# Grouped-query scores of a fusion model: four row groups of TensorE instead of block-diagonal keys

## The chip, the cores and the metric

The kernel runs on one core of one Trainium2 chip. The metric is the device time of one launch in microseconds; where several executions are given it is their median. Beside it stands one execution taken with the profiler.

## What is computed

A model of four layers over 32 sequences of 68 tokens (36 image patches and 32 text tokens), 256 wide, all in float32. Each layer has a mixing block and a feed-forward block, each behind a layer norm and with a residual sum. The change touches the mixing block of the last layer, grouped-query attention with 16 query heads and 4 key and value heads of 16 dimensions. Its core in the reference:

```python
Q = (x @ Wq.T).reshape(B, S, HKV, G, HEAD_DIM)
K = (x @ Wk.T).reshape(B, S, HKV, HEAD_DIM)
V = (x @ Wv.T).reshape(B, S, HKV, HEAD_DIM)
...
scores = jnp.einsum('bskgd,bswkd->bskgw', Q, K_win) * scale
...
attn = jax.nn.softmax(scores, axis=-1)
out = jnp.einsum('bskgw,bswkd->bskgd', attn, V_win)
return out.reshape(B, S, HQ * HEAD_DIM) @ Wo.T
```

The window reaches 128 tokens to both sides, more than the 68 there are, so each token sees all of its sequence and nothing is masked.

After it come the router and the dense expert block of the last layer.

## The kernel before, in words

There are five engine programs that meet only at semaphores. TensorE's order of steps is written out by a planner: `step(...)` puts a step into `pe_order`, and `Banks.plan` gives each result one of the eight PSUM banks in turn and notes which semaphore count frees that bank; `wait_free` waits for it. The ring `A` has banks 0 to 5, `B` 6 and 7, `W8` all eight.

Sequences ("batches") are grouped in five chunks of 7, 7, 6, 6 and 6. For each chunk `kv3` (L1043) and `q3_` (L1058) form keys, values and queries for all its batches; ScalarE copies them out of PSUM (`keep_kv3`, `keep_q3`, L1342 and L1360). Heads are padded from 16 to 32 rows, so that the four key heads fill 128 partitions, and the four queries of each key head stand side by side: 4 x 68 = 272 queries for each key head. Keys go into `kblk`, a block-diagonal tile: for each batch 4 x 68 columns of which head g fills only rows 32g to 32g+31, and the rest is zero, set once by GpSimd.

For each batch b:

1. `s3` (L1064, matmul at L1070): the 272 queries are cut into three pieces of 91 (from 0, 91 and 181, so the last two overlap by one). One matmul for each piece, 91 x 272, contracts over all 128 rows, for all four heads at once, because of the zeros in `kblk`. Each has a bank of ring `A`.
2. `shift3` on VectorE (L1862 to L1870): for each piece the maximum over the 68 keys (L1867), and the subtraction (L1868) into `p3`.
3. `exp3` on ScalarE (L1371), `sum3` on VectorE (sum L1876, reciprocal L1877), and GpSimd multiplies by the reciprocal (L2007).
4. `pT3_` (L1074, transposes at L1079): twelve transposes on TensorE; ScalarE copies each piece into `pT3` (a helper at L1130).
5. `pv3` (L1083, matmul at L1089): four matmuls, one for each key head, on column groups of the array (`tile_position=(0, g * HPAD)`); ScalarE copies the result (`keep_o3`).
6. `out3` at a chunk's end (helper at L759) multiplies by the output weights; VectorE adds to `h` and starts the layer norm.

`AHEAD` is 3, and `p3` has four slots. The orders of the turn b: TensorE does pT3(b), s3(b+3), pv3(b), with the projections of the next chunk or `out3` between at some turns. ScalarE does keep_o3(b-1), the three copies of pT3(b), exp3(b+3). VectorE does shift3(b+3), sum3(b+2). GpSimd works in order of b. Each float32 matmul is two passes in the trace, a transpose is one.

Of the kernel before, what the change touches and what calls it, by code (L numbers as in the profile page):

```python
# [13 lines left out]
P = 128  # L14
D = 256
HALVES = D // P
BATCH = 32
# [44 lines left out]
PROWS = 91  # L62
PIECE0 = [0, 91, 181]
AHEAD = 3

# [33 lines left out]
def build(nc, t, out):  # L99
# [3 lines left out]
    with ExitStack() as ctx:  # L103
# [197 lines left out]
        kblk = carve(KR * KV_HEADS * SEQ).rearrange("p (b g s) -> p b g s", g=KV_HEADS, s=SEQ)  # L301
# [42 lines left out]
        AB = Banks(psum, [0, 1], tenants)  # L344
        Q = Banks(psum, [0, 1, 2, 3], tenants)
# [7 lines left out]
        ln_ring = {L0A: F, L0F: Q, L1A: Q, L3A: W8}  # L353
# [183 lines left out]
        def plan_qkv3(c):  # L537
            A.plan(("k3", c), (sem("k3_kept"), c + 1))
            for j in range(V3[c]):
                A.plan(("v3", c, j), (sem("v3_kept"), V30[c] + j + 1))  # L540
            step("kv3", c)
            for j in range(GROUP):
                A.plan(("q3", c, j), (sem("q3_kept"), GROUP * c + j + 1))
# [13 lines left out]
        for b in range(BATCH + 1):  # L557
            if b in FEED3:
                plan_qkv3(FEED3[b])
            if b < BATCH:  # L560
                for i in range(PIECES):
                    A.plan(("pT3", b, i), (sem("pT3_kept"), PIECES * b + i + 1))
                step("pT3", b)
            if b + AHEAD < BATCH:
                plan_s3(b + AHEAD)
            if b and (b == BATCH or b in CHUNK_B0):
                c = CHUNKS - 1 if b == BATCH else CHUNK_B0.index(b) - 1
                plan_h("out3", L3A, c)
                plan_ln_after(L3F, c, 2)
            if b < BATCH:  # L570
                B.plan(("o3", b), (sem("o3_kept"), b + 1))
                step("pv3", b)
# [150 lines left out]
        def _(pe):  # L723
# [319 lines left out]
            def kv3(c):  # L1043
# [3 lines left out]
                dst = A.wait_free(pe, ("k3", c))  # L1047
                product(dst[:, 0:ntok(c)], lambda k: wk3[:, k, :], lambda k: xn[:, k, chunk(c)],
                        HALVES).then_inc(sem("k3_done"), 1)
                for j in range(V3[c]):  # L1050
                    dst = A.wait_free(pe, ("v3", c, j))
# [6 lines left out]
            def q3_(c):  # L1058
                for j in range(GROUP):
                    dst = A.wait_free(pe, ("q3", c, j))  # L1060
# [3 lines left out]
            def s3(b):  # L1064
                c = chunk_of[b]
                pe.wait_ge(sem("q3_kept"), GROUP * (c + 1))
                pe.wait_ge(sem("k3_kept"), c + 1)
                for i in range(PIECES):
                    dst = A.wait_free(pe, ("s3", b, i))
                    pe.matmul(dst[0:PROWS, 0:KV_HEADS * SEQ],  # L1070
                              q3[:, c % 2, b - CHUNK_B0[c], PIECE0[i]:PIECE0[i] + PROWS], kblk[:, at3(b)],
                              start=True, stop=True).then_inc(sem("s3_done"), 1)

            def pT3_(b):  # L1074
                pe.wait_ge(sem("p3_ready"), b + 1)
                for i in range(PIECES):
                    dst = A.wait_free(pe, ("pT3", b, i))
# [5 lines left out]
            def pv3(b):  # L1083
                c = chunk_of[b]
                pe.wait_ge(sem("v3_kept"), V30[c + 1])
                dst = B.wait_free(pe, ("o3", b))
# [6 lines left out]
            def out3(c):  # L1093
                pe.wait_ge(sem("o3_kept"), CHUNK_B0[c] + CHUNK_BATCHES[c])
                into_h("out3", wo3, lambda k, cols: oT3[:, k, cols], c, GROUP)
# [11 lines left out]
        def _(act):  # L1107
# [232 lines left out]
            act.wait_ge(sem("pool_setup"), 6)  # L1340

            def keep_kv3(c):  # L1342
                act.wait_ge(sem("k3_done"), c + 1)
                if c >= 2:
                    act.wait_ge(sem("s3_done"), PIECES * CHUNK_B0[c - 1])
                    act.wait_ge(sem("o3_done"), CHUNK_B0[c - 1])
                src = A.at(("k3", c))
                for g in range(KV_HEADS):
                    rows = slice(g * HPAD, (g + 1) * HPAD)
                    ins = act.activation(kblk[rows, at3(CHUNK_B0[c]):at3(CHUNK_B0[c]) + CHUNK_BATCHES[c], g, :],  # L1350
                                         seqs(src[rows, 0:ntok(c)]), ACT.Copy)
                ins.then_inc(sem("k3_kept"), 1)
                for j in range(V3[c]):
# [3 lines left out]
                    copy(vb3[0:SEQ, at3(b):at3(b) + n, :], A.at(("v3", c, j))[0:SEQ, 0:n * P].rearrange("p (b n) -> p b n", n=P),  # L1357
                         "v3_kept")

            def keep_q3(c):  # L1360
                for j in range(GROUP):
                    act.wait_ge(sem("q3_done"), GROUP * c + j + 1)
                    if c >= 2 and j == 0:
                        act.wait_ge(sem("s3_done"), PIECES * CHUNK_B0[c - 1])
                    copy(q3[:, c % 2, 0:CHUNK_BATCHES[c], j * SEQ:(j + 1) * SEQ], seqs(A.at(("q3", c, j))[:, 0:ntok(c)]),
                         "q3_kept")

            def exp3(b):
                act.wait_ge(sem("s3_shifted"), PIECES * (b + 1))
# [3 lines left out]
            def keep_o3(b):  # L1373
# [4 lines left out]
                     B.at(("o3", b))[:, 0:GROUP * SEQ].rearrange("p (j t) -> p j t", j=GROUP), "o3_kept")  # L1378

            keep_kv3(0)  # L1380
            keep_q3(0)
            for b in range(AHEAD):
                exp3(b)
            for b in range(BATCH + 1):
# [7 lines left out]
                for i in range(PIECES):  # L1392
# [3 lines left out]
                         A.at(("pT3", b, i))[0:SEQ, 0:KV_HEADS * PROWS].rearrange("p (g q) -> p g q",  # L1396
                                                                                 g=KV_HEADS)[:, :, -lap:PROWS],
# [10 lines left out]
        def _(dve):  # L1408
# [691 lines left out]
```

## Time and profile before

| | |
|---|---|
| median of 3 runs | 1849.72 us (1848.54 to 1851.34) |
| profiled execution | 1853.17 us |
| its span, first to last instruction | 1851.4 us |
| TensorE busy over the span | 1680.1 us, 91% |
| VectorE busy | 798.7 us, 43% |
| ScalarE busy | 498.6 us, 27% |
| GpSimd busy | 418.0 us, 23% |
| the last attention block | about 1494.8 to 1702.8 us of the span |

The shares are means over some twenty stages with different limits. The block of the change is about an eleventh of the span, so it has to be read by itself, from the timeline and the tables of stretches. PE is TensorE's matmuls, PEld its loads of weights, which run beside them. A matmul's own duration holds its latency; of matmuls in a row the distance between two starts is the price.

### The profile page before, as it was taken

The numbers are of one execution on the slowest core, as the hardware profiler recorded it, in microseconds if no ns is written. First come the engines' busy times: TensorE is split into PE (matmuls) and PEld (weight loads), VectorE is DVE, ScalarE is ACT, GpSimd is POOL, SyncE is SP. The second block draws the span as 40 slices with busy tenths as digits, with TensorE's granted clock in tenths as the row PEclk, the third lists the DMA queues.
The fourth block names the chain that finished last, engine by engine and source line by source line (L and its number), as shares of the span: only waits on it lengthen the run. The fifth ranks groups of instructions, "written<-read, shape, count | busy, mean of one in ns | idle before, by whom it ended". The sixth has DMA issues, their size and how long they took to land.

```text
span 1851.4 us, 22690 instructions
## 1 busy us (share of the span) xinstructions
PE 1680.1 (91%) x8028; PEld 1167.6 (63%) x8028; DVE 798.7 (43%) x1698; ACT 498.6 (27%) x962; POOL 418.0 (23%) x430
## 2 busy tenths in 40 slices
PE   5877499988999999999949999999899989998999
PEld 4532134437999999999935555776864456667444
DVE  3531499987111111111126760122456555675455
ACT  1234344541212221212116323123110035543000
POOL 0363577771111111211121000000100012232000
PEclk8989799997899999999989979999579999998999
DMA  5233434434344344404161000010000010000000
GB/s 168 66 94 95 110 106 96 101 71 150 146 160 175 150 160 159 162 28 160 33 182 39 1 1 28 1 46 1 1 1 0 1 46 1 1 1 1 12 17 20
DMA packets 59046, 129.17 MB, mean 70 GB/s; under 512 B 10563, under 2 KB 39268, under 8 KB 52388
## 3 DMA queue, kind: packets, MB, share of 16 engines
q1 hardware_dynamic: 54996, 116.96, 19.8%
q0 software_dynamic: 3936, 10.75, 1.7%
q8 instruction: 64, 1.05, 0.2%
q14 instruction: 50, 0.41, 0.1%
HBM read 196.35 MB, written 9.97 MB: 111 GB/s over the span
## 4 chain that ended last, share of the span: by engine, by line
PE 75%; DVE 10%; SPq 5%; issue 4%; POOL 3%; ACT 2%; DMA 1%; DVEq 0%; ACTq 0%; POOLq 0%
PE psum L727 39%; PE psum L1030 13%; PE psum L759 7%; PE psum L822 4%; SPq L627 3%; DVE work L1734 3%; PE psum L737 2%; PE psum L1009 2%; PE psum L938 2%; DVE work L1868 1%; SPq L624 1%; DVE work L1867 1%; POOL xn L1937 1%; ACT work L1130 1%; PE psum L1039 1%
## 5 line engine op out<-in xcount | busy, mean ns | idle before, releaser
L727 PE MATMUL psum<-work 128*128 128x128 f32 (+3 forms) x3400 | 470.4, 300 | 16.1 <-DMA work<-in_xp 15.9
L727 PEld LDWEIGHTS psum<-work 128*128 128x128 f32 x3400 | 440.0, 193 | 33.5 <-DMA work<-in_xp 15.9
L1030 PE MATMUL psum<-w_late,xn 128*128 128x512 f32 x544 | 242.0, 603 | 0.0
L1801 DVE TENSOR_TENSOR work<-sq,psum 128x512 f32<-128x512 f32 x82 | 56.3, 687 | 387.3 <-PE psum L727 387.3
L1030 PEld LDWEIGHTS psum<-w_late,xn 128*128 128x128 f32 x544 | 103.5, 193 | 128.6 <-issue 119.2
L822 PE MATMUL psum<-work,xn 128*128 128x408 f32 (+1 forms) x320 | 152.9, 591 | 31.9 <-POOL work L1959 31.4
L1734 DVE TENSOR_TENSOR_SCAN work<-psum,work 128x414 f32<-128x414 f32 (+1 forms) x160 | 158.8, 1058 | 43.2 <-POOL work L1959 38.9
L1959 POOL TENSOR_TENSOR work<-work 128x408 f32<-128x408 f32 (+1 forms) x160 | 160.9, 1039 | 58.0 <-PE psum L822 29.6
L1918 POOL TENSOR_TENSOR rs<-rs,power 128x4 f32<-128x4 f32 (+3 forms) x40 | 44.6, 1115 | 547.2 <-DVE rs L1428 540.9
L1618 DVE SCALAR_TENSOR_TENSOR h<-psum,gate,h 128x256 f32<-128x256 f32 x272 | 119.4, 480 | 106.8 <-PE psum L1030 104.1
L1130 ACT ACTIVATE work<-psum 68x364 f32<-68x364 f32 (+10 forms) x256 | 108.0, 463 | 139.5 <-PE psum L727 57.5
L822 PEld LDWEIGHTS psum<-work,xn 128*128 128x128 f32 x320 | 55.2, 200 | 125.3 <-POOL work L1959 81.1
L1225 ACT ACTIVATE psum<-work,a_neg 128x408 f32<-128x408 f32 (+1 forms) x160 | 100.3, 627 | 122.6 <-DVE work L1734 122.6
L1985 POOL DMA_INDIRECT y_rows<-sq,row_of x41 | 40.5, 987 | 367.0 <-ACT sq L1130 367.0
L1464 DVE TENSOR_TENSOR h<-h,psum 128x512 f32<-128x512 f32 (+1 forms) x45 | 29.4, 654 | 159.1 <-PE psum L759 122.8
L1126 ACT ACTIVATE xn<-psum 128x512 f32<-128x512 f32 (+1 forms) x63 | 34.4, 574 | 224.9 <-PE psum L737 224.7
L1267 ACT ACTIVATE sq<-psum 128x512 f32<-128x512 f32 x82 | 49.0, 597 | 161.1 <-PE psum L727 161.0
L938 PE MATMUL psum<-w_attn 128*128 128x512 f32 x128 | 62.4, 632 | 22.2 <-POOL w_attn L1928 22.2
L2007 POOL TENSOR_TENSOR work<-work 91x816 f32<-91x816 f32 x32 | 49.5, 1548 | 139.3 <-DVE work L1877 139.3
L727 PE MATMUL psum<-work,w_attn 128*128 128x408 f32 (+1 forms) x200 | 74.3, 531 | 2.5 <-ACT work L1123 2.5
L1130 ACT ACTIVATE sq<-psum 128x256 f32<-128x256 f32 x41 | 15.7, 383 | 185.8 <-PE psum L727 185.8
L737 PE MATMUL psum<-ident,sq 128*128 128x128 f32 x238 | 43.7, 332 | 24.3 <-DVE sq L1449 23.6
(266 smaller groups left out, 2052.9 us busy)
## 6 DMA issues: line engine op xcount, KB each, us to landing
work<-in_W SPq DMA_DIRECT2D x123, 1024.0 KB
work<-c_rows SPq DMA_DIRECT2D x48, 204.0 KB, 3.1
w_attn<-in_B SPq DMA_DIRECT2D x64, 128.0 KB, 2.4
work<-c_rows SPq DMA_DIRECT2D x32, 238.0 KB, 3.2
w_attn<-in_A SPq DMA_DIRECT2D x64, 64.0 KB, 2.2
w_attn<-in_A SPq DMA_DIRECT2D x32, 128.0 KB, 2.5
work<-in_A SPq DMA_DIRECT2D x32, 128.0 KB, 2.5
work<-y_rows SPq DMA_DIRECT2D x8, 512.0 KB, 7.8
```

The source lines that it names most:

```text
L727: mm = pe.matmul(dst, lhs(k), rhs(k), start=(k == 0), stop=(k == parts - 1))
L737: tr = pe.transpose(dst[:, at:at + P], src[:, k * P:(k + 1) * P], ident[:])
L759: mm = pe.matmul(cols, lhs(k, slice(i * P, (i + 1) * P)), w[:, k, :], start=(k == 0), stop=(k == parts - 1 and bias is None))
L822: pe.matmul(dst[:, 0:ntok(c)], diag[:, m, n, :], ym[:, g % RING, 0:ntok(c)], start=(n == 0), stop=(n == N_STATE - 1)).then_inc(sem("y_adde ...
L938: mm = pe.matmul(banks[m], unit_short(i)[:, m * P:(m + 1) * P], unit_long(i), start=first_mm, stop=last_mm)
L1030: mm = pe.matmul(dst.rearrange("p (e n) -> p e n", e=2), xn[:, k, i * P:(i + 1) * P], w_last[:, 2 * q:2 * q + 2, k, :], start=(k == 0), st ...
L1130: act.activation(dst, src, ACT.Copy).then_inc(sem(signal), 1)
L1225: act.activation(dst[:, :, 1:SEQ + 1], seqs(dtx[:, m, chunk(c)]), ACT.Exp, scale=a_neg[:, m, n:n + 1]).then_inc(sem("decay"), 1)
L1618: dve.scalar_tensor_tensor(h[:, i], W8.at(("dx", r, i, q))[:, e * D:(e + 1) * D], gate[:, 5, i, 2 * q + e:2 * q + e + 1], h[:, i], ALU.mul ...
L1734: dve.tensor_tensor_scan(f_buf[:, g % RING, 0:N], AB.at(("a", g))[:, 0:N], added, 0.0, ALU.mult, ALU.add).then_inc(sem("scanned"), 1)
L1801: dve.tensor_tensor(hm[:, j % 2, 4 * q:4 * q + 4, :].rearrange("p k n -> p (k n)"), sa[:, i % 2], A.at(("e3", j, q)), ALU.mult).then_inc(s ...
L1959: pool.tensor_tensor(seqs(ym[:, g % RING, 0:ntok(c)]), f[:, :, 1:SEQ + 1], seqs(cbr[:, k % CRING, 0:ntok(c)]), ALU.mult).then_inc(sem("y_p ...
```

## The change

Keys aren't block-diagonal any more: `kblk` becomes `k3`, 128 rows by the tokens of a chunk, twice, with 28 spare columns, and one copy fills it instead of four. Scores are twelve matmuls a batch instead of three: for each of three pieces and each of four key heads, 32 rows (a row group of the array, `tile_position=(g * HPAD, 0)`), 96 queries by 96 columns of keys. Of the 96 columns the first 68 are the batch's own; the others are the next batch's or spare and aren't read. Each key head has a bank of its own, in which the three pieces stand side by side. Pieces begin at 0, 96 and 176.

The banks are dealt anew: `S4` has banks 0 to 3 for scores, `T` 4 to 6 for projections, transposes and output, `O` bank 7 for the value products. A score set takes all of `S4`, and is freed as a whole when its subtraction is over. VectorE does one maximum and one subtraction for a batch, over 4 banks. ScalarE's turn b ends with exp3(b+2) and not exp3(b+3), and VectorE's turn b is sum3(b+1), shift3(b+3). The early layer norms of the last block get banks 4 and 5.

```diff
-PROWS = 91
-PIECE0 = [0, 91, 181]
+PROWS = 96
+PIECE0 = [0, 96, 176]
 AHEAD = 3
+KEYS = 96
...
-        kblk = carve(KR * KV_HEADS * SEQ).rearrange("p (b g s) -> p b g s", g=KV_HEADS, s=SEQ)
+        k3 = carve(2 * (NMAX + KEYS - SEQ)).rearrange("p (r t) -> p r t", r=2)
...
+        S4 = Banks(psum, [0, 1, 2, 3], tenants)
+        T = Banks(psum, [4, 5, 6], tenants)
+        O = Banks(psum, [7], tenants)
...
-        ln_ring = {L0A: F, L0F: Q, L1A: Q, L3A: W8}
+        ln_ring = {L0A: F, L0F: Q, L1A: Q, L3A: W8, L3F: Banks(psum, [4, 5], tenants)}
...
         def plan_s3(b):
-            for i in range(PIECES):
-                A.plan(("s3", b, i), (sem("s3_shifted"), PIECES * b + i + 1))
+            for g in range(KV_HEADS):
+                S4.plan(("s3", b, g), (sem("s3_shifted"), b + 1))
...
+                banks = [S4.wait_free(pe, ("s3", b, g)) for g in range(KV_HEADS)]
                 for i in range(PIECES):
-                    dst = A.wait_free(pe, ("s3", b, i))
-                    pe.matmul(dst[0:PROWS, 0:KV_HEADS * SEQ],
-                              q3[:, c % 2, b - CHUNK_B0[c], PIECE0[i]:PIECE0[i] + PROWS], kblk[:, at3(b)],
-                              start=True, stop=True).then_inc(sem("s3_done"), 1)
+                    for g in range(KV_HEADS):
+                        rows = slice(g * HPAD, (g + 1) * HPAD)
+                        k0 = (b - CHUNK_B0[c]) * SEQ
+                        mm = pe.matmul(banks[g][0:PROWS, i * KEYS:(i + 1) * KEYS],
+                                       q3[rows, c % 2, b - CHUNK_B0[c], PIECE0[i]:PIECE0[i] + PROWS],
+                                       k3[rows, c % 2, k0:k0 + KEYS],
+                                       start=True, stop=True, tile_position=(g * HPAD, 0))
+                mm.then_inc(sem("s3_done"), 1)
...
-                src = A.at(("k3", c))
-                for g in range(KV_HEADS):
-                    rows = slice(g * HPAD, (g + 1) * HPAD)
-                    ins = act.activation(kblk[rows, at3(CHUNK_B0[c]):at3(CHUNK_B0[c]) + CHUNK_BATCHES[c], g, :],
-                                         seqs(src[rows, 0:ntok(c)]), ACT.Copy)
-                ins.then_inc(sem("k3_kept"), 1)
+                copy(k3[:, c % 2, 0:ntok(c)], T.at(("k3", c))[:, 0:ntok(c)], "k3_kept")
...
-            for b in range(AHEAD):
+            for b in range(AHEAD - 1):
                 exp3(b)
...
-                if b + AHEAD < BATCH:
-                    exp3(b + AHEAD)
+                if b + AHEAD - 1 < BATCH:
+                    exp3(b + AHEAD - 1)
...
             def shift3(b):
-                for i in range(PIECES):
-                    dve.wait_ge(sem("s3_done"), PIECES * b + i + 1)
-                    s = A.at(("s3", b, i))[0:PROWS, 0:KV_HEADS * SEQ].rearrange("p (g s) -> p g s", g=KV_HEADS)
-                    mx = st3[0:PROWS, b % (AHEAD + 1), 0, i * KV_HEADS:(i + 1) * KV_HEADS]
-                    link(dve.tensor_reduce(mx, s, AX_X, ALU.max))
-                    dve.tensor_tensor(p3[0:PROWS, b % (AHEAD + 1), i], s,
-                                      mx.unsqueeze(2).to_broadcast([PROWS, KV_HEADS, SEQ]),
-                                      ALU.subtract).then_inc(sem("s3_shifted"), 1)
+                dve.wait_ge(sem("s3_done"), b + 1)
+                s = psum[0:PROWS, S4.bank["s3", b, 0]:S4.bank["s3", b, 0] + KV_HEADS, 0:PIECES * KEYS].rearrange(
+                    "p g (i s) -> p i g s", i=PIECES)[:, :, :, 0:SEQ]
+                mx = st3[0:PROWS, b % (AHEAD + 1), 0, :].rearrange("p (i g) -> p i g", i=PIECES)
+                link(dve.tensor_reduce(mx, s, AX_X, ALU.max))
+                dve.tensor_tensor(p3[0:PROWS, b % (AHEAD + 1)], s,
+                                  mx.unsqueeze(3).to_broadcast([PROWS, PIECES, KV_HEADS, SEQ]),
+                                  ALU.subtract).then_inc(sem("s3_shifted"), 1)
...
-            shift3(0)
-            for b in range(1, AHEAD):
+            for b in range(AHEAD):
                 shift3(b)
-                sum3(b - 1)
+            sum3(0)
             for b in range(BATCH + 1):
+                if b + 1 < BATCH:
+                    sum3(b + 1)
                 if b + AHEAD < BATCH:
                     shift3(b + AHEAD)
-                if b + AHEAD - 1 < BATCH:
-                    sum3(b + AHEAD - 1)
```

## Rows read from the trace of the kernel before

**Rows 1.** Table by stretches: stretch, its length, busy us (count) of each engine, PEclk.
```profile
1572.50:1600.40 27.90, 25.39 (x189) 17.64 (x187) 23.16 (x55) 13.96 (x31) 9.29 (x6) 1.00 0.01 1
1600.40:1610.00 9.60, 9.60 (x48) 6.41 (x45) 1.25 (x5) 4.47 (x9) 0.00 (x0) 1.00 0.00 0
```

**Rows 2.** Grouped lines by shape, 1500 us to the end: count, busy us, mean ns.
```profile
L1070 PE MATMUL psum<-work 128*91 128x272 f32 x192 | 50.4, 401 | 0.7 <-ACT work L1130 0.7
L2007 POOL TENSOR_TENSOR work<-work 91x816 f32<-91x816 f32 x32 | 49.5, 1548 | 139.3 <-DVE work L1877 139.3
L1868 DVE TENSOR_TENSOR work<-psum,work 91x272 f32<-91x272 f32 x96 | 41.9, 437 | 3.3
L1867 DVE TENSOR_REDUCE work<-psum 91x4 f32<-91x272 f32 x96 | 40.3, 420 | 54.5 <-PE psum L1070 54.5
...
L1876 DVE TENSOR_REDUCE work<-work 91x12 f32<-91x816 f32 x32 | 31.6, 986 | 0.0
L1070 PEld LDWEIGHTS psum<-work 128*91 128x91 f32 x192 | 28.8, 163 | 11.2 <-ACT work L1130 1.4 <-issue 0.7
```

**Rows 3.** TensorE's timeline over one period of six batches: start us, us, what.
```profile
1572.54 1.11 PE L1079 MATMUL psum<-ident,work 91*68 91x91 f32 x12
...
1575.55 1.13 PE L1079 MATMUL psum<-ident,work 91*68 91x91 f32 x12
...
1579.70 1.14 PE L1079 MATMUL psum<-ident,work 91*68 91x91 f32 x12
...
1590.47 1.13 PE L1079 MATMUL psum<-ident,work 91*68 91x91 f32 x12
...
1610.03 1.10 PE L1079 MATMUL psum<-ident,work 91*68 91x91 f32 x12
```

**Rows 4.** Timeline of all engines over one batch in the middle of a chunk.
```profile
1549.23 0.67 PE L1089 MATMUL psum<-work 68*32 68x272 f32 x8 [0.52 <-ACT work L1130]
...
1549.83 1.13 PE L1079 MATMUL psum<-ident,work 91*68 91x91 f32 x12
...
1550.80 1.54 PE L1070 MATMUL psum<-work 128*91 128x272 f32 x6
...
1551.33 0.22 DVE L1877 RECIPROCAL work<-work 91x12 f32<-91x12 f32 x1
1551.47 0.42 DVE L1867 TENSOR_REDUCE work<-psum 91x4 f32<-91x272 f32 x1
1551.63 1.55 POOL L2007 TENSOR_TENSOR work<-work 91x816 f32<-91x816 f32 x1 [2.02 <-DVE work L1877]
...
1552.80 0.67 PE L1089 MATMUL psum<-work 68*32 68x272 f32 x8 [0.47 <-ACT work L1130]
```

**Rows 5.** Timeline of TensorE's weight loads in the same batch.
```profile
1549.20 0.19 PEld L1089 LDWEIGHTS psum<-work 68*32 68x32 f32 x8 [0.95 <-issue]
1549.83 0.93 PEld L1079 LDWEIGHTS psum<-ident,work 91*68 91x68 f32 x12 [0.44 <-POOL work L2007]
```

**Rows 6.** Timeline of all engines at the start of the block.
```profile
1506.70 4.36 PE L1070 MATMUL psum<-work 128*91 128x272 f32 x18 [0.66 <-ACT work L1130]
...
1512.36 0.99 DVE L1876 TENSOR_REDUCE work<-work 91x12 f32<-91x816 f32 x1
...
1515.29 2.03 PE L1079 MATMUL psum<-ident,work 91*68 91x91 f32 x12 [4.22 <-POOL work L2007]
```

**Rows 7.** Table by stretches, columns as in rows 1: a batch, thin stretches, the tail.
```profile
1542.00:1553.00 11.00, 9.51 (x82) 6.05 (x86) 10.59 (x25) 6.73 (x15) 4.88 (x4) 1.00 0.01 1
1576.00:1579.40 3.40, 2.35 (x23) 1.50 (x21) 3.26 (x9) 2.24 (x5) 1.47 (x1) 1.00 0.02 5
1679.75:1682.20 2.45, 1.73 (x20) 1.08 (x20) 2.38 (x6) 1.26 (x3) 1.39 (x3) 0.96 0.00 0
1682.30:1695.90 13.60, 10.77 (x57) 6.89 (x58) 0.86 (x2) 4.89 (x12) 2.91 (x2) 0.51 0.00 1
```

More of the change, by code:

```diff
@@ L561, in build @@
                 for i in range(PIECES):
-                    A.plan(("pT3", b, i), (sem("pT3_kept"), PIECES * b + i + 1))
+                    T.plan(("pT3", b, i), (sem("pT3_kept"), PIECES * b + i + 1))
                 step("pT3", b)
@@ L567, in build @@
                 c = CHUNKS - 1 if b == BATCH else CHUNK_B0.index(b) - 1
-                plan_h("out3", L3A, c)
+                plan_h("out3", L3A, c, T)
                 plan_ln_after(L3F, c, 2)
             if b < BATCH:
-                B.plan(("o3", b), (sem("o3_kept"), b + 1))
+                O.plan(("o3", b), (sem("o3_kept"), b + 1))
                 step("pv3", b)
@@ L1046, in kv3 @@
                 wait_normed(pe, L3A, c)
-                dst = A.wait_free(pe, ("k3", c))
+                dst = T.wait_free(pe, ("k3", c))
                 product(dst[:, 0:ntok(c)], lambda k: wk3[:, k, :], lambda k: xn[:, k, chunk(c)],
@@ L1050, in kv3 @@
                 for j in range(V3[c]):
-                    dst = A.wait_free(pe, ("v3", c, j))
+                    dst = T.wait_free(pe, ("v3", c, j))
                     for i in range(4 * j, min(4 * j + 4, CHUNK_BATCHES[c])):
@@ L1059, in q3_ @@
                 for j in range(GROUP):
-                    dst = A.wait_free(pe, ("q3", c, j))
+                    dst = T.wait_free(pe, ("q3", c, j))
                     product(dst[:, 0:ntok(c)], lambda k: wq3[:, k, j, :], lambda k: xn[:, k, chunk(c)],
@@ L1076, in pT3_ @@
                 for i in range(PIECES):
-                    dst = A.wait_free(pe, ("pT3", b, i))
+                    dst = T.wait_free(pe, ("pT3", b, i))
                     for g in range(KV_HEADS):
@@ L1085, in pv3 @@
                 pe.wait_ge(sem("v3_kept"), V30[c + 1])
-                dst = B.wait_free(pe, ("o3", b))
+                dst = O.wait_free(pe, ("o3", b))
                 pe.wait_ge(sem("pT3_kept"), PIECES * (b + 1))
@@ L1094, in out3 @@
                 pe.wait_ge(sem("o3_kept"), CHUNK_B0[c] + CHUNK_BATCHES[c])
[L1095 removed]
+                into_h("out3", wo3, lambda k, cols: oT3[:, k, cols], c, GROUP, T)
             steps = {"ln": ln, "hT": hT, "tok": tok, "prims": prims, "guards": guards, "z": z, "dt": dt, "yacc": yacc,
@@ L1356, in keep_kv3 @@
                     act.wait_ge(sem("v3_done"), V30[c] + j + 1)
-                    copy(vb3[0:SEQ, at3(b):at3(b) + n, :], A.at(("v3", c, j))[0:SEQ, 0:n * P].rearrange("p (b n) -> p b n", n=P),
+                    copy(vb3[0:SEQ, at3(b):at3(b) + n, :], T.at(("v3", c, j))[0:SEQ, 0:n * P].rearrange("p (b n) -> p b n", n=P),
                          "v3_kept")
@@ L1363, in keep_q3 @@
                     if c >= 2 and j == 0:
-                        act.wait_ge(sem("s3_done"), PIECES * CHUNK_B0[c - 1])
-                    copy(q3[:, c % 2, 0:CHUNK_BATCHES[c], j * SEQ:(j + 1) * SEQ], seqs(A.at(("q3", c, j))[:, 0:ntok(c)]),
+                        act.wait_ge(sem("s3_done"), CHUNK_B0[c - 1])
+                    copy(q3[:, c % 2, 0:CHUNK_BATCHES[c], j * SEQ:(j + 1) * SEQ], seqs(T.at(("q3", c, j))[:, 0:ntok(c)]),
                          "q3_kept")
             def exp3(b):
-                act.wait_ge(sem("s3_shifted"), PIECES * (b + 1))
+                act.wait_ge(sem("s3_shifted"), b + 1)
                 v = p3[0:PROWS, b % (AHEAD + 1)]
@@ L1377, in keep_o3 @@
                 copy(oT3[:, :, b * SEQ:(b + 1) * SEQ],
-                     B.at(("o3", b))[:, 0:GROUP * SEQ].rearrange("p (j t) -> p j t", j=GROUP), "o3_kept")
+                     O.at(("o3", b))[:, 0:GROUP * SEQ].rearrange("p (j t) -> p j t", j=GROUP), "o3_kept")
+            act.wait_ge(sem("pool_setup"), 6)
             keep_kv3(0)
             keep_q3(0)
-            for b in range(AHEAD):
+            for b in range(AHEAD - 1):
                 exp3(b)
@@ L2001, in _ @@
             wait_all(pool, L2F)
-            pool.memset(kblk, 0.0).then_inc(sem("pool_setup"), 1)
+            pool.memset(k3, 0.0).then_inc(sem("pool_setup"), 1)
             ln(L3A)
```

13 lines of the change are left out of this document (6 added, 7 removed).

## The prediction

> **What bounds the kernel now.** I read the table by stretches first. Only the last attention block is touched, and it repeats two kinds of stretch: one that holds the batches' own steps, where TensorE is busy for 25.39 of 27.9 us and VectorE for 23.16, and one with the key, value and query products, where TensorE never rests and VectorE works 1.25 of 9.6 us [rows 1]. So TensorE is the bound between the groups of batches and two engines are close inside them.
>
> Then the grouped lines for the price of each step [rows 2], and TensorE's timeline for how a period of six batches is spent [rows 3]: from 1572.54 to 1610.03 is 37.5 us; the first batch takes 3.01, the second 4.15, the next three together 10.77 (3.59 each), and 19.56 us pass from the last transposes of the period to the first of the next.
>
> Last, one batch on all engines [rows 4]. Transposes, scores, then a wait of 0.47 to 0.52 us for ScalarE's copies, then the value products; 3.57 us from value product to value product. VectorE goes without a rest: the exponentials' sum is followed at once by the next maximum. Its work per batch in starts is three times (0.46 + 0.355) for maximum and subtraction, 1.02 + 0.15 for sum and reciprocal, together 3.6. The exponential also waits for the last subtraction, and ScalarE's copies queue behind it. So a batch costs 3.6 by VectorE, about 3.0 by TensorE (0.97 + 1.38 + 0.60).
>
> **The change part by part.**
> *Scores.* 192 matmuls are three products a batch, two passes each, one behind the other at (1.54 - 0.392) / 5 = 0.23 us for 272 columns (the x6 group of rows 3 and 4; the mean of 0.401 is latency): 1.38 us of TensorE [rows 2, 4]. Afterwards there are 12 products of 96 columns, 24 passes, in six rounds of four row groups. 96 columns at 0.23 / 272 are 0.081; transposes of 91 columns come at (1.13 - 0.242) / 11 = 0.081, scaled to 96 it is 0.085 [rows 4]. I take 0.083. Six rounds together are 0.50 us; one at a time 24 x 0.085 = 2.04. The nearest thing in the trace is the value product: four column groups, eight passes of 272 columns, all in 0.67 us where a single pass takes some 0.4 [rows 4], so groups of columns run together. Its eight loads, each 0.106 us, all fit into 0.19 [rows 5]: the loads overlap too. These are column groups, and row groups are in no row, so both ends stay: 0.50 and 2.04. I take 0.50, since the value product is nearer to it in kind.
> By the Trainium skill, "TensorE: Matmul & The Clock Gate", "Measured speedup vs the span model", four row tiles gained 3.07x on products of 512 columns, not 4x. By that figure my estimate would be 2.0 / 3.07 = 0.65 us and the gain some 2 us smaller; no run here shows it.
> *Change of array layout.* The value product ends its columns at 0.6 us but the next transposes follow 0.1 us later than columns alone explain. Scores now need such a change as well: +0.1 a batch on TensorE, between 0 and 0.2.
> *Pieces of 96.* Twelve transposes of 96 instead of 91 columns: 12 x 0.085 = 1.02 against 0.97, +0.05. The three copies behind them hold 384, 384 and 320 instead of 364, 364 and 360 columns: the sum is the same.
> *VectorE.* One maximum and one subtraction over 816 columns replace three of each. From the rows 0.426 and 0.437 for 272 columns and 0.986 for 816 [rows 2], 544 more columns cost 0.56 to 0.57: maximum 0.99 + 0.03 to its dependent subtraction, next start 0.93 after that. So 1.95 instead of 2.45 us, and with the sum 3.12 instead of 3.6. The read now crosses four banks in runs of 68 of 96; at worst that costs 0.1 each, at best nothing.
> *One batch behind.* ScalarE no longer waits for the subtraction that has just been issued, so its copies are free of it. In exchange the sum of batch b+1 is asked for one turn later than now, just before POOL's multiplication (1.55) and the transposes that want it. This slack is used up: a new loop closes.
> *Banks.* Scores have four banks in one set instead of their share of six: the scores of b+1 can't start before the subtraction of b is over. Transposes and projections have three banks. A projection takes about 1.4 us on TensorE and its copy 0.5, so three are enough: 0, at most 0.2 a period. The key copy shrinks from four to one; ScalarE waits for TensorE there, so 0.
>
> **The new loop**, over two batches: reciprocal 0.22, to POOL 0.08, multiplication 1.55, to TensorE 0.06, transposes 1.02, layout 0.1, scores 0.50 + 0.18 until the last has landed, to VectorE 0.05, maximum 1.02, subtraction 0.93, next sum 1.02: 6.73, or 3.37 a batch. VectorE alone is 3.12. So the steady batch goes from 3.59 to about 3.4, and not to 3.1: what is late next is POOL's result.
>
> **The sum.** For a period of six batches: first batch 2.8 (TensorE and the copies), second 4.1 (its wait for ScalarE stays), then 3.1 to 3.7 in turn, on average 3.3: 2.8 + 4.1 + 9.9 = 16.8 against 17.93, so -1.1. In the last piece transposes and scores are 1.74 instead of 2.35: -0.6. A period: -1.7 to -1.8. There are three such, and one of seven batches: -2.3 there. Together -7.7.
> Start: now three score sets go out at once and the first transposes start at 1515.29 [rows 6]. After, each set waits for the subtraction before it: 0.1 + 0.68 + 0.1 + 0.05 = 0.95 plus 2.0 a turn. First maximum at 1507.4, three subtractions end at 1515.4, sum 1516.6, POOL 1518.2: transposes at 1518.3, +3.0. While TensorE is idle there its clock goes to the low level; at that level each score set gives back about 1.8 us. Two of them are at it: +1.5 net, between 0 and +3.
> Tail: the last three batches have no scores, -1.2, between -3 and 0.
> Sum: -7.7 + 1.5 - 1.2 = **-7.4 us**. The profiled execution took 1853.17 us with a span of 1851.4; the sum off the span gives 1844.0. The median of three runs is 1849.72, some 3.5 us below the profiled one, and against it the forecast is **1842.3**. What follows (the router and dense blocks) is untouched.
>
> **The rivals.**
> (A) *Row groups run together*, as above: 1842 (1835 to 1846). Chance 0.50.
> (B) *They overlap by half*: 1.0 us a score set. The loop gets 6.73 + 0.5 = 7.2, 3.6 a batch, what it is now; with the start +3 and small gains between: 1849 (1846 to 1852). A worse price on banks or VectorE's runs lands here too, and so does a change that moves nothing. For it: no row shows row groups. Against: the value product's 0.67. Chance 0.17.
> (C) *The loads of weights go one after another*, since every row group fills the same columns. Today a load of 91 columns hides behind 272 streamed ones: 0.163 against 0.23 of pitch [rows 2]; after it stands against 96. Place: between transposes and value product. Price 2.04 instead of 1.38: loop 6.73 - 0.50 + 2.04 = 8.3, 4.1 a batch against 3.6. 20 such batches: +10; the 12 others, bound by TensorE, +0.8 each: +10; start +3 + 4: 1849.7 + 27 = 1876. It turns the sign from a set of about 1.1 us. Against it: eight loads in 0.19 [rows 5]. Chance 0.10.
> (D) *The low clock.* TensorE worked 9.51 of 11 us at a batch now, after it is (1.02 + 0.1 + 0.5 + 0.6 + some 0.2) / 3.4, some 70%. A stretch at 2.35 of 3.4 kept clock 1.00, one at 1.73 of 2.45 was followed by 0.51 for 13.6 us [rows 7]. At the low level the loop has 1.02 + 0.5 more, +0.8 a batch; if half of some 24 batches run so: -7.4 + 10 = +3, 1853 (1848 to 1860). Chance 0.14.
> The same page of the Trainium skill ("A second HAM failure mode: psum-queue depth-cycling") tells of a kernel whose TensorE paused so often between groups that its clock swung between both levels; the trace of before shows no such swing inside the batches.
> (E) *More than the sum*: the clock stays high at start and tail: 1836 (1832 to 1838). Chance 0.09.
>
> **How the numbers follow.** The likeliest is (A), 1842.3. The range leaves out (C) and the far ends of (D) and (E): **1835 to 1858**; (A) alone has 1835 to 1846. About 0.2%, 3.7 us, is what a measurement of this kernel can tell from no change. Faster: (A) 0.46, (E) 0.09, a bit of (B) 0.02: 0.57. Same: (A) 0.04, (B) 0.12, (D) 0.03: 0.19. Slower: (C) 0.10, (D) 0.11, (B) 0.03: 0.24.
>
> **What would show it.** Of each set, 24 matmuls of 32 rows inside about 0.7 us (A), 1.2 (B) or 2.2 (C). Steps of 3.1 and 3.7 us in turn between transposes, VectorE with short rests before the maximum, transposes that wait for POOL. First transposes at about 1518.3 on the clock of the trace. Granted clock 1.00 from the first query products to the last scores; anything less is (D). The forecast is wrong if VectorE's maximum over four banks takes well over 1.0 us, or if the 0.1 us of the layout change is several times that.

## The result, and the profile after

The changed kernel takes 1866.84 us, the median of four runs (1865.79 to 1869.45), against 1850.53 of the kernel before beside it: a ratio of 1.0086, 95% interval 1.0065 to 1.0107. It is 16 us slower; 7.4 us less had been forecast. The profiled execution took 1865.85 us with a span of 1864.1.

The first scores start at 1506.70 us of the span before and at 1502.55 after. What comes ahead of them is unchanged and moves by some us from one execution to the next (in the traces of all kernels here the first scores start between 1497 and 1507 us). So the traces are compared from the first scores on: 344.7 us before, 361.6 after. (The block of the change is 208 of the 1851 us before, a ninth of the span.)

The grouped lines of the changed kernel from 1500 us on answer to [rows 2] (shape and count, then busy us and mean ns of one):

```profile
L1088 PE MATMUL psum<-ident,work 96*68 96x96 f32 x384 | 50.7, 297 | 16.0 <-POOL work L2010 15.9
L2010 POOL TENSOR_TENSOR work<-work 96x816 f32<-96x816 f32 x32 | 49.5, 1550 | 152.5 <-DVE work L1881 152.5
...
L1872 DVE TENSOR_TENSOR work<-psum,work 96x816 f32<-96x816 f32 x32 | 32.1, 1003 | 1.1
L1871 DVE TENSOR_REDUCE work<-psum 96x12 f32<-96x816 f32 x32 | 32.0, 1000 | 73.9 <-PE psum L1077 73.8
...
L1077 PE MATMUL psum<-work 32*96 32x96 f32 x768 | 30.8, 302 | 7.4 <-DVE work L1872 6.8 <-ACT work L1139 0.7
```

Scores fell from 50.4 to 30.8 us busy, maximum and subtraction from 82.2 to 64.1. Each step became as cheap as it was meant to. But transposes rose from 39.1 to 50.7 us, far more than five columns in 91. Their line in the kernel before, over the same part:

```profile
L1079 PE MATMUL psum<-ident,work 91*68 91x91 f32 x384 | 39.1, 256 | 4.2 <-POOL work L2007 4.2
```

The reason stands in the last column but two of the table by stretches, the granted clock (stretch, length, busy of the five engines, clock, share of DMA, GB/s):

```profile
1543.50:1559.50 16.00, 15.71 (x168) 11.40 (x168) 11.21 (x15) 9.67 (x19) 5.76 (x5) 0.53 0.00 1
1576.81:1612.91 36.10, 31.85 (x342) 22.89 (x341) 22.48 (x35) 17.45 (x37) 9.30 (x6) 1.00 0.01 2
1612.91:1655.35 42.44, 40.62 (x342) 29.37 (x341) 23.77 (x39) 18.33 (x37) 10.26 (x7) 0.76 0.01 1
1714.80:1731.90 17.10, 17.10 (x75) 15.48 (x75) 3.29 (x11) 2.78 (x5) 0.21 (x1) 0.51 0.00 0
```

Rows two and three are two periods of six batches with the same work. One ran at 2.4 GHz and took 36.1 us, less than the 37.5 of [rows 3]. In the other the clock fell to 1.2 GHz after two batches and stayed there for 20.5 us: 42.4 us. From the first scores on, the low level (1.2 GHz; the profile shows it as a granted clock of 0.5) holds 95.6 us after and 30.7 before.

TensorE's timeline shows both kinds of batch, high first (start us, us, what, wait and releaser):

```profile
1586.98 1.18 PE L1088 MATMUL psum<-ident,work 96*68 96x96 f32 x12 [0.67 <-POOL work L2010]
1588.10 0.76 PE L1077 MATMUL psum<-work 32*96 32x96 f32 x24
1588.87 0.67 PE L1098 MATMUL psum<-work 68*32 68x272 f32 x8
1590.59 1.18 PE L1088 MATMUL psum<-ident,work 96*68 96x96 f32 x12 [1.05 <-POOL work L2010]
...
1624.20 2.13 PE L1088 MATMUL psum<-ident,work 96*68 96x96 f32 x12
1626.26 1.29 PE L1077 MATMUL psum<-work 32*96 32x96 f32 x24
1627.49 1.14 PE L1098 MATMUL psum<-work 68*32 68x272 f32 x8
1628.55 2.13 PE L1088 MATMUL psum<-ident,work 96*68 96x96 f32 x12
```

At the high level TensorE waits for GpSimd's result ahead of the transposes of the four batches in the middle of a period, and a batch takes 3.23 and 3.61 us in turn. At the low level its own work is 4.35 us a batch, and there it doesn't wait. In the batch of [rows 4] it waited too, but 0.5 us of 3.6, and kept its clock.

The 16.9 us from the first scores on, by stretch (differences of the two timelines; low: us at the low level; the last output product is the last of the matmuls that form the block's output):

| stretch | before (low) | after (low) | difference |
|---|---|---|---|
| first scores to first transposes | 8.6 (0.5) | 12.7 (8.3) | +4.1 |
| batches 0 and 1 | 20.2 (6.3) | 21.5 (12.1) | +1.4 |
| batches 2 to 8 | 37.1 (0) | 40.0 (17.1) | +3.0 |
| 9 to 14 | 37.5 (0) | 36.1 (0) | -1.4 |
| 15 to 20 | 37.5 (0) | 42.4 (20.5) | +4.9 |
| 21 to 26 | 25.4 (0) | 24.5 (0) | -0.9 |
| 27 to the last output product | 29.6 (13.6) | 31.2 (20.5) | +1.6 |
| from there to the end | 148.8 (10.2) | 153.0 (17.1) | +4.2 |

### The profile page after: what moved, and what is told of

Same layout as the page of the kernel before. It is cut to its first block, busy times and chain, and to the rows that moved or that the text cites. A ratio compares the mean times of both kernels' runs of the same rounds, so it can differ in the third digit from the quotient of the medians.

```text
span 1864.1 us, 23763 instructions
## 1 busy us (share of the span) xinstructions
PE 1686.5 (90%) x8604; PEld 1177.5 (63%) x8604; DVE 784.9 (42%) x1570; ACT 495.7 (27%) x947; POOL 416.6 (22%) x430
## 4 chain that ended last, share of the span: by engine, by line
PE 76%; DVE 9%; SPq 5%; issue 4%; POOL 3%; ACT 2%; DMA 1%; DVEq 0%; ACTq 0%; POOLq 0%
PE psum L731 39%; PE psum L1034 13%; PE psum L763 7%; PE psum L826 4%; SPq L631 3%; DVE work L1738 3%; PE psum L1088 2%; PE psum L741 2%; PE psum L1013 2%; PE psum L942 2%; PE psum L1077 1%; SPq L628 1%; POOL xn L1940 1%; PE psum L1043 1%; DMA work<-in_txt 1%
## 5 line engine op out<-in xcount | busy, mean ns | idle before, releaser
L731 PE MATMUL psum<-work 128*128 128x128 f32 (+3 forms) x3400 | 470.1, 300 | 15.1 <-DMA work<-in_xp 15.1
L731 PEld LDWEIGHTS psum<-work 128*128 128x128 f32 x3400 | 439.8, 193 | 32.3 <-DMA work<-in_xp 15.1
L1139 ACT ACTIVATE work<-psum 68x384 f32<-68x384 f32 (+11 forms) x261 | 116.5, 468 | 214.4 <-PE psum L731 93.2
L2010 POOL TENSOR_TENSOR work<-work 96x816 f32<-96x816 f32 x32 | 49.5, 1550 | 152.5 <-DVE work L1881 152.5
L741 PE MATMUL psum<-ident,sq 128*128 128x128 f32 x238 | 44.7, 337 | 24.6 <-DVE sq L1453 22.7
L1088 PE MATMUL psum<-ident,work 96*68 96x96 f32 x384 | 50.7, 297 | 16.0 <-POOL work L2010 15.9
```

The costliest lines, as they stand in the source:

```text
L731: mm = pe.matmul(dst, lhs(k), rhs(k), start=(k == 0), stop=(k == parts - 1))
L741: tr = pe.transpose(dst[:, at:at + P], src[:, k * P:(k + 1) * P], ident[:])
L1088: tr = pe.transpose(dst[0:SEQ, g * PROWS:(g + 1) * PROWS], p3[0:PROWS, b % (AHEAD + 1), i, g, :], ident[0:PROWS, 0:PROWS])
L1139: act.activation(dst, src, ACT.Copy).then_inc(sem(signal), 1)
```

## The experiments

All of them compute the same scores, softmax and output; where matmuls are added nothing reads their results. One execution of each kernel has a trace. Extra matmuls, as I call them below, are two float32 products of 128x128 by 128 columns, four passes.

**1. Extra matmuls in the gap.** Theory 1: the low clock comes from too thin work of TensorE in the batches and is the loss. Theory 2: it is a by-product, and scores on row groups or the new loop lose the time.

```diff
             def pT3_(b):
+                dst = T.wait_free(pe, ("pT3", b, 0))
+                for _ in range(2):
+                    pe.matmul(dst[:, 384:512], wo3[:, 0, 0:P], wo3[:, 1, 0:P], start=True, stop=True)
                 pe.wait_ge(sem("p3_ready"), b + 1)
```

> The changed kernel with two more matmuls of 128x128 by 128 columns (0.43 us at the high clock, their result is overwritten) where TensorE waits for GpSimd before each batch's transposes. Theory 1 (the granted clock fell because TensorE did too little in the batches, and that is the whole loss): the clock stays 1.00 between the batches, a period of six batches takes 36 to 36.5 us in all chunks, and the kernel takes 1840 to 1848 us. Theory 2 (the low clock is a by-product; scores on row groups or the new loop lose the time): the period stays at 40 to 42 us wherever it was, and 0.43 us a batch comes on top, 1867 to 1880 us.

1855.14 us, the median of ten, a ratio to before of 1.0018 (1.0004 to 1.0033); against 1866.84 this is 12 us less, for adding work. The mean granted clock over the whole kernel was 0.925 to 0.931 in these ten executions and 0.912 to 0.915 in the four of the changed kernel.

```profile
1577.51:1613.91 36.40, 35.23 (x367) 26.02 (x366) 22.47 (x35) 17.52 (x38) 9.29 (x6) 1.00 0.01 2
1613.91:1650.31 36.40, 35.24 (x367) 26.04 (x365) 23.77 (x39) 17.52 (x38) 10.25 (x7) 1.00 0.01 2
1704.90:1857.60 152.70, 147.90 (x418) 75.11 (x416) 72.42 (x168) 6.14 (x12) 1.95 (x2) 0.94 0.05 15
```

Both periods take 36.4 us at clock 1.00; the one that took 42.4 is gone. Between the third transposes and the last scores no low clock is left. Theory 1 holds for the batches. But it also said that this is the whole loss, and it isn't: the start (12.7 us) and the end (the third row; 153.0 from the last output product) are as long as in the changed kernel, so the time ends 7 us above the 1848 of the range.

**2. The same on the kernel before**, in its own gap, ahead of the value products:

```diff
                 dst = B.wait_free(pe, ("o3", b))
+                pe.matmul(dst[:, 384:512], wo3[:, 0, 0:P], wo3[:, 1, 0:P], start=True, stop=True)
+                pe.matmul(dst[:, 384:512], wo3[:, 0, 0:P], wo3[:, 1, 0:P], start=True, stop=True)
                 pe.wait_ge(sem("pT3_kept"), PIECES * (b + 1))
```

> The kernel before with the same two extra matmuls, put where TensorE waits before each batch's value products. Control for the run above: before had its clock at 1.00 in the batches, so theory 1 expects nothing there, 0 to +4 us from batches without a wait, and perhaps -3 to 0 at the tail where the clock was low: 1846 to 1855 us. If extra matmuls helped the kernel before by as much as the changed one, the theory would be about something that both kernels have.

1846.83 us, ratio 0.9974 (0.996 to 0.9988): 5 us less than the kernel before beside it (1852.18), more than expected, against 12 us in the changed kernel. In its trace the periods get 0.35 us longer (37.8 us), and the last five batches with the output products take 24.6 instead of 29.6 us, with no low clock instead of 13.6 us of it. So theory 1 holds at the tail, where the kernel before had the low clock. But that trace doesn't show a gain of 5 us in the total: the batches ahead got 2.8 us longer, the end 1.6 us (15.1 us of low clock there instead of 10.2), and from the first scores to the end it is 344.1 us against 344.7. Where the 5 us between the medians come from is open.

**3. and 4. Columns streamed**, `KEYS = 68` and `KEYS = 160` instead of 96.

> The changed kernel with 68 columns streamed by each score product instead of 96, nothing else. Theory 1: fewer columns make TensorE's work thinner, so the clock is low for the same time or longer: same or slower, 1866 to 1880 us. Theory 2 (time is lost by what the score set costs): a set takes 0.76 us or less and each batch gains up to 0.15 us: 1860 to 1865 us. If the set still takes 0.76 us, loads of 96 columns are its price, not the columns streamed.

> The changed kernel with 160 columns streamed by each score product instead of 96: six rounds of 0.137 instead of 0.083 us, 0.32 us more in the loop over two batches. Theory 1: the added columns keep the clock high in most batches, which gives back more than 0.16 us a batch costs: 1848 to 1858 us. Theory 2: it is slower than the changed kernel by 32 times 0.16 to 0.32 us, 1872 to 1877 us.

68 columns: 1872.89 us, ratio 1.0113 (1.0077 to 1.0148). 160 columns: 1861.68 us, 1.006 (1.004 to 1.0081). Two periods of the first, one of the second:

```profile
1578.72:1619.89 41.17, 39.11 (x341) 28.14 (x340) 22.47 (x35) 18.11 (x37) 9.29 (x6) 0.79 0.01 1
1619.89:1660.96 41.07, 39.02 (x341) 28.08 (x340) 23.76 (x39) 18.11 (x37) 10.26 (x7) 0.79 0.01 1
...
1569.40:1606.75 37.35, 33.40 (x342) 23.97 (x341) 22.48 (x35) 17.45 (x37) 9.29 (x6) 1.00 0.01 2
```

With fewer columns all periods contain the low clock. With more columns none does in the one execution with a trace (1856.25 us), and each set costs more (1.07 us against 0.76). None of the nine executions reached the 1872 us of theory 2; the slowest took 1868.11. Whether the useless columns made the kernel faster isn't shown: the median is 5 us lower, but the two intervals overlap, four of the nine lie in the range of the changed kernel, and 1861.68 lies above theory 1's 1858. With 68 columns a set still takes 0.74 us against 0.76:

```profile
1579.93 0.74 PE L1077 MATMUL psum<-work 32*96 32x68 f32 x24
```

So between 68 and 96 columns the price of a set isn't the columns streamed but what else goes with 24 passes; that it is the loads of 96 columns, as the expectation had it, no run separates. From 96 to 160 columns the streaming counts: 0.31 us more.

**5. Scores back to block-diagonal keys**, all else as changed, but for the keys' copy, which is four parts again.

```diff
                 for i in range(PIECES):
-                    for g in range(KV_HEADS):
...
+                    mm = pe.matmul(banks[i][0:PROWS, 0:KV_HEADS * SEQ],
+                                   q3[:, c % 2, b - CHUNK_B0[c], PIECE0[i]:PIECE0[i] + PROWS], kblk[:, at3(b)],
+                                   start=True, stop=True)
```

> The changed kernel with its scores put back to three products of 128 rows by 272 columns on block-diagonal keys (banks, one maximum and one subtraction, and the exponential's turn stay as changed). Theory 1 (shorter score sets are what makes TensorE's work too thin): the clock stays 1.00 between batches; the set costs 1.38 instead of about 0.6 us, so the loop over two batches has 0.8 us more and a period of six batches takes 37.5 to 38.5 us, like before: 1850 to 1858 us, faster than the changed kernel. Theory 3 (the new order with its waits for GpSimd makes the clock fall, whatever the scores are): the clock falls here too and the time is 1868 us or more.

1872.63 us, ratio 1.012 (1.01 to 1.0139). A period, and a batch in it:

```profile
1578.66:1618.52 39.86, 36.45 (x233) 24.57 (x232) 22.47 (x35) 18.88 (x40) 9.29 (x6) 1.00 0.00 1
...
1586.27 1.18 PE L1084 MATMUL psum<-ident,work 96*68 96x96 f32 x12 [0.30 <-POOL work L2011]
1587.81 1.59 PE L1074 MATMUL psum<-work 128*96 128x272 f32 x6 [0.36 <-DVE work L1873]
1589.33 0.67 PE L1094 MATMUL psum<-work 68*32 68x272 f32 x8
```

On the clock theory 1 was right: 1.00 in every period, and 0.925 to 0.929 over the whole kernel in all four executions. Theory 3 was wrong about it, though the time is the one that it named. On the time theory 1 was wrong by 15 us: 39.9 us a period, not 37.5 to 38.5, and 16.7 us from the first scores to the first transposes. The single score set makes TensorE wait for VectorE's subtraction (0.36) besides GpSimd (0.30), and a batch takes 4.03 us. The one set of banks and the new turn lose 2.4 us a period against before; at the high clock the short sets on row groups pay for that and 1.4 us more. Not separated by any run: whether the clock falls because the sets are short, or because their products use row groups instead of the full array.

**6. The exponential's turn undone**, with the extra matmuls: ScalarE's `exp3(b + AHEAD)` behind the copies of b, VectorE's `shift3(b + AHEAD)` ahead of `sum3(b + AHEAD - 1)`. The first sums go back between the first subtractions with it.

> The changed kernel with the extra matmuls of the first run (so that the clock stays high in the batches) and with the exponential and the sums in the turns that they had before (exponential of b+3 behind the copies of b, sum of b+2). If the earlier turn is what it gains by, a period of six batches takes 37 us instead of 36.4 and the kernel 3 to 6 us more than with the extra matmuls alone. If the loop through GpSimd's multiplication holds the batches up more than the exponential would, it is the same or faster by 1 to 3 us.

1864.63 us, ratio 1.0077 (1.0057 to 1.0098), against 1855.14 with the turn as changed. A period at high clock takes 38.4 us instead of 36.4 (expected 37). So the earlier turn is worth 2 us a period, three times what was expected. Batches 2 to 8 fell to the low clock for 23.9 us, and another period for 3.4, in spite of the extra matmuls, so part of the 9.5 us in the total is clock; the start gave back 3.7 us (9.0 us to the first transposes instead of 12.7).

**7. Four batches ahead**, with the extra matmuls and sums two turns early.

```diff
-AHEAD = 3
+AHEAD = 4
...
+            sum3(1)
             for b in range(BATCH + 1):
-                if b + 1 < BATCH:
-                    sum3(b + 1)
+                if b + 2 < BATCH:
+                    sum3(b + 2)
```

> The changed kernel with the extra matmuls, with scores four batches ahead instead of three and the sum of b+2 instead of b+1 in VectorE's turn b, so that the loop through GpSimd spans one batch more. The forecast named that loop as what is late next (3.37 us a batch) and VectorE as the bound behind it (3.12): a steady batch should take 3.1 to 3.25 us and a period of six 35.3 to 36 us instead of 36.4, 2 to 4 us in all. If the loop isn't the bound, the period stays at 36.4.

1849.66 us, ratio 1.0005 (0.9988 to 1.0022), against 1.0018 for the first experiment. VectorE's timeline in a batch:

```profile
1591.08 1.00 DVE L1874 TENSOR_REDUCE work<-psum 96x12 f32<-96x816 f32 x1
...
1592.12 1.00 DVE L1875 TENSOR_TENSOR work<-psum,work 96x816 f32<-96x816 f32 x1
...
1593.04 0.99 DVE L1883 TENSOR_REDUCE work<-work 96x12 f32<-96x816 f32 x1
...
1594.07 0.22 DVE L1884 RECIPROCAL work<-work 96x12 f32<-96x12 f32 x1
...
1594.31 1.00 DVE L1874 TENSOR_REDUCE work<-psum 96x12 f32<-96x816 f32 x1
```

It works without rest and a batch is 3.23 us, a period 35.3 to 35.6. TensorE's waits for GpSimd ahead of the transposes come to 3.8 us where the changed kernel had 15.9. The loop through GpSimd was what held the batches up, and VectorE is the bound behind it. The start got longer, 16.5 us from first scores to first transposes, by a fourth round of scores and subtraction.

**8. and 9. Banks of the last layer norms.** From the third on they get banks 0 to 5; with the extra matmuls, and alone.

```diff
+        late = Banks(psum, [0, 1, 2, 3, 4, 5], tenants)
+        class Split(Banks):
+            def plan(self, key, freed_by):
+                if key[2] < 2:
+                    super().plan(key, freed_by)
+                else:
+                    late.plan(key, freed_by)
+                    self.bank[key], self.before[key] = late.bank[key], late.before[key]
...
-        ln_ring = {L0A: F, L0F: Q, L1A: Q, L3A: W8, L3F: Banks(psum, [4, 5], tenants)}
+        ln_ring = {L0A: F, L0F: Q, L1A: Q, L3A: W8, L3F: Split(psum, [4, 5], tenants)}
```

> The changed kernel with the extra matmuls and with the last layer norms (from the third on) on banks 0 to 5 instead of 4 and 5. From the last output product to the end the changed kernel takes 152.97 us where before took 148.77. If two banks for the layer norms are the reason, this comes back to 149 to 150 us and the kernel gains 3 to 4 us; if the clock falls there for its own reasons, it stays at 152 to 153.

> The changed kernel without extra matmuls, with the last layer norms (from the third on) on banks 0 to 5. The run with the extra matmuls took 147.1 us from the last output product to the end with this edit and 153.0 without it. If the two banks are the whole reason for the longer end, the changed kernel gains 4 to 6 us by this alone, 1861 to 1863 us, and its batches still show the low clock.

With the extra matmuls: 1849.09 us, ratio 0.9977 (0.9958 to 0.9996), 6 us under the first experiment, more than expected; the end takes 147.1 us instead of 153.0. In the changed kernel a layer norm waits for the bank of an output tile that VectorE has yet to add (first fence), with six banks none waits (second):

```profile
1713.43 0.65 PE L741 MATMUL psum<-ident,sq 128*128 128x128 f32 x4 [0.79 <-DVE h L1468]
```

```profile
1703.08 0.64 PE L751 MATMUL psum<-ident,sq 128*128 128x128 f32 x4
```

0.8 us of waiting isn't 4 us. The rest is the clock: in the changed kernel the clock fell 3.5 us into this stage and was low for 17.1 us, over the logits and the first dense products (last row of the table by stretches); before, it was low for 10.2, with six banks 6.8. The stretch has no rest, so 6.9 us more at half clock cost about 3.4 us by my estimate, 4.2 with the wait. Over all traces the end takes 153.0 to 154.7 us in the seven kernels with two banks, each with at least 17.1 us of low clock, and 147.1 to 152.1 in the five with six banks. One of these five (run 11) has 17.1 us of low clock at the same place without the wait, so the wait isn't the only thing that the clock falls for. Alone, in the changed kernel, the edit took the end to 148.8 us, but the kernel took 1866.14 us instead of the expected 1861 to 1863, ratio 1.0083 (1.0062 to 1.0104), which can't be told from the changed kernel: in its profiled execution a third group of batches (21 to 26) had the low clock, 29.3 us instead of 24.5. So the shorter end is shown; that the edit alone makes the kernel faster isn't.

**10. to 12. Putting it together.** The first sums go into the gaps between the first subtractions (10), scores four ahead with that (11), and ten further extra products behind each of the first four score sets (12).

```diff
-            for b in range(AHEAD):
+            shift3(0)
+            for b in range(1, AHEAD):
                 shift3(b)
-            sum3(0)
+                sum3(b - 1)
             for b in range(BATCH + 1):
-                if b + 1 < BATCH:
+                if b and b + 1 < BATCH:
                     sum3(b + 1)
```

And for (12):

```diff
                 mm.then_inc(sem("s3_done"), 1)
+                if b < AHEAD:
+                    dst = T.wait_free(pe, ("pT3", 0, 0))
+                    for _ in range(10):
+                        pe.matmul(dst[:, 384:512], wo3[:, 0, 0:P], wo3[:, 1, 0:P], start=True, stop=True)
```

> Extra matmuls, layer norms on six banks, and in addition the first sums in the gaps between the first subtractions (sum of b-1 behind the subtraction of b, as before) instead of behind the third. VectorE waits there for score sets anyway, so the first transposes should start 2 to 3 us earlier after the first scores (12.7 us now, 8.6 before): 1845 to 1848 us, by 2 to 3 us under the run without this edit.

> The run before with scores four batches ahead instead of three (sums two turns early). A period of six batches takes 35.4 us instead of 36.4, and the fourth score set at the start costs up to 3.3 us more. If only the start keeps it from paying, it comes out within 1 us of the run before; with the start's sums in the gaps it should be 0 to 2 us faster: 1843 to 1847 us.

> The same with ten more extra matmuls (about 1.1 us at the high clock) behind each of the first four score sets, where TensorE waits for VectorE. If the low clock over the first batches (8 to 13 us of it) comes from TensorE's waits there, it goes or shrinks below 4 us, and the first two batches take 18.5 to 19.5 us instead of 21 to 22.8: 1840 to 1844 us.

(10): the start shrank as expected and a little more, from 12.7 to 8.9 us. The total didn't follow: 1850.9 us, ratio 1.0001 (0.9986 to 1.0016), above the 1845 to 1848 expected. In its trace the low clock held 10.2 us of the last batches and output products, where run 8 had none. (11): 1840.74 us, 0.9947 (0.9928 to 0.9966), 10 us under (10) where 0 to 2 were expected. Its trace is of the slowest of its four executions (1847.05) and shows 3.3 us less than that of (10) from the first scores on; what gave the rest is open. (12): 1839.81 us, **0.9946 (0.9925 to 0.9967)**: faster than both kernels, by 10 us than before and by 27 than the changed one. Not faster than (11) by what the medians can tell. Its start:

```profile
1504.04 2.50 PE L1095 MATMUL psum<-w_attn 128*128 128x128 f32 x20
1506.58 0.76 PE L1087 MATMUL psum<-work 32*96 32x96 f32 x24
...
1516.51:1533.56 17.05, 17.02 (x146) 11.37 (x145) 4.71 (x8) 8.43 (x17) 3.10 (x2) 1.00 0.00 1
1569.14:1604.69 35.55, 34.46 (x366) 26.02 (x365) 22.65 (x33) 17.52 (x37) 9.29 (x6) 1.00 0.01 1
```

Ten products take 2.5 us, not 1.1 as the expectation had it. They fill the wait, the clock is 1.00 from the first scores to the last output product, and the first two batches take 17.1 us where the changed kernel takes 21.5 (18.5 to 19.5 expected).

## Why the prediction was wrong

*What held.* Row groups run together: 24 passes in 0.76 us with their latency against 0.68 in the sum. The change of layout costs about 0.1 us: transposes to scores takes 1.12 us for 1.02 of columns. Maximum and subtraction over four banks take 1.000 and 1.003 us (forecast 0.99 and 1.00). The new loop through GpSimd's multiplication: 3.42 us a batch at high clock against 3.37, in steps of 3.23 and 3.61 against 3.1 and 3.7. The seventh experiment shows that it was this loop. A period at high clock is 36.1 us where the sum had 35.7. Rivals (B) and (C), half overlap and serial loads, fall by the 0.76 us.

By the Trainium skill's figure of 3.07x ("TensorE: Matmul & The Clock Gate", "Measured speedup vs the span model") I estimated 0.65 us for the passes. The trace gives 0.59 (0.76 less some 0.17 of latency), so this case lies between that figure and a factor of four.

*The step that failed* is the one that the forecast put as "Granted clock 1.00 from the first query products to the last scores", with a chance of 0.14 for rival (D), the low clock. The runs showed the low clock for 95.6 us instead, 37.6 of them in batches 2 to 20. The sum took 0.9 us a batch of score passes off an engine that already waited, and priced what was left at the high level. The trace of before had the warning: the thin stretch that was followed by the low clock [rows 7]. I set the stretch that had kept its clock beside it and gave the fall a small chance. Also (D)'s price was too low. It had 0.8 us a batch; the measured difference is 4.35 less 3.42, 0.93, and it came as whole stretches of 17 to 20 us that reached over the output products too (9.05 us instead of 7.17). But what took the measured time beyond (D)'s 1848 to 1860 is mostly the start, the tail and the end, below: 11 of the 14 us between (D)'s sum and the traces.

*Start:* forecast +1.5, measured +5.5. First transposes were +4.1 instead of +3.0 late, since a round of scores and subtraction takes 3.23 us, not 2.95, and the third score set already ran at the low level (1.29 us instead of 0.76). The give-back at the low level did come (1.29 us a score set against 2.93; 1.8 had been forecast), but in the first two batches the low clock lasted 12.1 instead of 6.3 us and took it away again. The tenth experiment shows that the late start is VectorE's order: the first sum behind the third subtraction.

*Tail and end:* forecast -1.2, measured +1.6, and +4.2 behind it where the text said "What follows (the router and dense blocks) is untouched". It isn't. The diff gives all layer norms of the last block two banks, not only the early ones as the section on the change has it, and I put that edit at nothing without looking at who holds these banks. They are the output tiles' banks. The eighth experiment shows the wait (0.8 us) and, with six banks, an end that is 5.9 us shorter. The larger part is the clock, and that the wait makes it fall is likely, not shown.

*Periods:* forecast -7.7. At high clock they give -1.4 for each of two groups of six batches, -0.9 for the third, which has no projections in it, and -1.1 for the seven (as in the first experiment, with its extra matmuls), -4.8 in all. With the low clock the changed kernel has +3.0, -1.4, +4.9 and -0.9: +5.6.

The trace agrees with the Trainium skill where it was cited beside (D) ("TensorE: Matmul & The Clock Gate", "A second HAM failure mode: psum-queue depth-cycling"): the clock swung between its two levels, five stretches of the low one in 226 us, as TensorE paused between groups. That the trace of before shows no swing holds for batches 2 to 26; it has one low stretch at the first two batches and one at the last. The extra matmuls, which fill just these pauses, took the swing out of batches 2 to 26 in all kernels but one (run 6).

*Still open:* which stretches fall. Two of four groups of batches did in the changed kernel's trace, three with the edit of experiment 9, all with 68 columns; two periods with the same work and the same waits went one each way in one execution. What decides it wasn't tried. Nor were extra matmuls placed ahead of the last value products and output products, where the low clock came and went between kernels with the same code there.

## What to carry to other kernels

Before work is taken off TensorE in a stage where it already waits, look for stretches of the same trace that are about as thin as the stage will be, and price the stage at both clock levels; a gain of 0.2 us a batch doesn't survive a stretch at half clock. Where the waits can't be removed, a few matmuls into a free part of a bank that TensorE owns at that moment cost little (0.3 us a period) and gave back 12 us here; in one kernel they didn't keep the clock up. And an edit that deals out banks is a wait until it is shown who held each bank last.

## What the runs showed of the hardware that was not expected

- Adding work made the kernel faster: six times 0.45 us a period of added passes took 12 us off the changed kernel. The kernel before, which had no low clock between its first two and its last batches, got 5 us faster by the medians, of which the trace shows the place but not the sum.
- Twelve float32 products of 32 rows, 96 stationary and 96 streamed columns on four row groups take 0.76 us, 0.74 with 68 streamed columns and 1.07 with 160: between 68 and 96 columns the streaming is not what counts.
- The time of one kernel can spread with its clock: with 160 columns nine executions took 1854 to 1868 us at mean granted clocks from 0.930 down to 0.921, against 1866 to 1869 us at 0.912 to 0.915 in four of the changed kernel. Which periods fell in each isn't known, since only one has a trace.
